# Three places in the instruction order of a gated-linear-attention and mixture-of-experts kernel: ScalarE's transposed input before the router's scale, its sixth chunk's heads before a scale, VectorE's keys before a normalised merge

## The reference

```
h  = layernorm(x)
q  = relu(h Wq)   16 heads of 64          k = relu(h Wk)   4 heads of 64      v = h Wv   4 heads of 64
g  = log_sigmoid(h Wg1 Wg2 + bg2) / 16    per key channel
S_t = exp(g_t) S_(t-1) + k_t v_t^T ;  o_t = (q_t / 8) S_t          (gated linear attention)
o  = g_norm_weight * o / rms(o) per head ;   x1 = x + layernorm(o Wo)
n  = layernorm(x1)
logits = n router_w^T + router_b ; the best 2 of 8 experts, gates = softmax of the two logits
y  = sum over the two experts e of gate_e * (silu(n gate_e^T) * (n up_e^T)) down_e^T
out = x1 + layernorm(y)
```

## Time and profile before

| | |
|---|---|
| time, median of 3 runs | 1233.63 us (1232.5 to 1234.02) |
| profiled execution, its time | 1234.89 us |
| its span, first to last instruction | 1233.1 us |
| mean granted TensorE clock | 0.983 |
| busy | PE 1159.7 us (94%), PEld 985.2 (80%), DVE 771.2 (63%), ACT 652.6 (53%), POOL 554.7 (45%) |
| first stage | to about 800 us, a turn every 48 us in the loop |

### The profile page before, as it was taken

The page is one execution under the profiler, slowest core; times in us unless marked ns, Lnnn a source line. Parts: engine busy times, 40 slices in busy tenths (PEclk is TensorE's granted clock), DMA queues, the critical chain, the costliest instruction groups (busy, mean ns, idle before and its releaser), DMA issues.

```text
span 1233.1 us, 29645 instructions
## 1 busy us (share of the span) xinstructions
PE 1159.7 (94%) x9166; PEld 985.2 (80%) x9166; DVE 771.2 (63%) x2380; ACT 652.6 (53%) x1653; POOL 554.7 (45%) x686
## 2 busy tenths in 40 slices
PE   8999999999999999999999999499999999999895
PEld 5878878878788788788788788379999999988762
DVE  5777777886887787777778868523333333333337
ACT  4755656557547557556565573334444444443336
POOL 2244464554654654644645544423333333333326
PEclk9999999999999999999999999689999999999998
DMA  7010110100101100101101001334111111111534
GB/s 280 10 28 14 30 43 9 34 28 24 34 17 30 38 17 26 43 13 30 43 9 34 28 15 43 135 106 116 49 46 51 49 45 51 47 48 43 175 118 189
DMA packets 59676, 67.50 MB, mean 55 GB/s; under 512 B 6896, under 2 KB 49664, under 8 KB 59264
## 3 DMA queue, kind: packets, MB, share of 16 engines
q1 hardware_dynamic: 48720, 41.10, 10.7%
q0 software_dynamic: 8448, 17.45, 4.3%
q10 hardware_dynamic: 2480, 8.61, 2.1%
HBM read 37.98 MB, written 29.15 MB: 54 GB/s over the span
## 4 chain that ended last, share of the span: by engine, by line
PE 65%; DVE 18%; issue 6%; ACT 6%; DMA 3%; DVEq 1%; POOL 0%; ACTq 0%; SPq 0%; POOLq 0%
PE pO L779 9%; PE pO L606 5%; PE pW L639 5%; PE pO L611 5%; PE pA L770 4%; PE pA L771 4%; PE pJ L770 4%; PE pJ L771 4%; PE pJ L561 3%; PE pA L590 3%; DVE qT L1133 3%; DVE ss L1181 3%; PE pJ L519 2%; PE pA L561 2%; PE pJ L639 2%
## 5 line engine op out<-in xcount | busy, mean ns | idle before, releaser
L1656 POOL DMA_INDIRECT expert_out<-y,tail x136 | 130.1, 957 | 263.3 <-ACT y L1038 239.8
L890 ACT ACTIVATE sq<-pO 128x512 f32<-128x512 f32 x128 | 75.8, 592 | 159.3 <-PE pO L606 109.0
L606 PEld LDWEIGHTS pO<-vJ,aT 128*128 128x128 f32 x1024 | 127.9, 192 | 27.0 <-issue 24.0
L606 PE MATMUL pO<-vJ,aT 128*128 128x128 f32 x1024 | 139.1, 279 | 5.5 <-DVE aT L1174 5.5
L1567 POOL DMA_INDIRECT expert_rows<-x1n,rowi x120 | 120.3, 1002 | 47.7 <-issue 29.5
L779 PE MATMUL pO<-wdown_sb,vJ 128*128 128x128 f32 x1088 | 134.1, 277 | 0.0
L1181 DVE TENSOR_REDUCE ss<-sq 128x8 f32<-128x512 f32 x128 | 86.4, 675 | 68.6 <-ACT sq L890 67.6
L779 PEld LDWEIGHTS pO<-wdown_sb,vJ 128*128 128x128 f32 x1088 | 128.4, 194 | 0.0
L1435 DVE TENSOR_TENSOR vJ<-pA,kJ 128x256 f32<-128x256 f32 x136 | 57.6, 425 | 108.3 <-ACT kJ L1027 108.3
L611 PE MATMUL pO<-S_mid,qT 128*128 128x128 f32 x896 | 118.3, 275 | 0.0
L611 PEld LDWEIGHTS pO<-S_mid,qT 128*128 128x128 f32 x896 | 109.1, 192 | 0.0
(11 more groups left out here) (234 smaller groups left out, 2422.5 us busy)
## 6 DMA issues: line engine op xcount, KB each, us to landing
xt<-expert_rows SPq DMA_DIRECT2D x69, 130.0 KB
xa<-x SPq DMA_DIRECT2D x16, 256.0 KB, 3.0
xr<-x SPq DMA_DIRECT2D x16, 256.0 KB, 2.9
after_attention<-x SPq DMA_DIRECT2D x16, 256.0 KB, 2.4
arena<-after_attention ACTq DMA_DIRECT2D x8, 512.0 KB
expert_rows<-zeros SPq DMA_DIRECT2D x8, 390.0 KB
expert_out<-y,tail POOLq DMA_INDIRECT x136
wgate_sb<-wgate SPq DMA_DIRECT2D x1, 2048.0 KB, 9.4
```

What stands on the lines that cost most here:

```text
L606: last = mm(o[:, g, h, :, :], aT[:, c % 2, h, g * P:(g + 1) * P], vJ[:, c, h, :], start=(h == 0 and g == 0), stop=(c == 0), skip_group_che ...
L1656: g.indirect_dma_start(out=ys_dram, in_=y[:, k, :], in_offset=None, out_offset=bass.IndirectOffsetOnAxis(ap=tail[:, k, 1:2].bitcast(U32), ...
```

## The change

Three edits, in the streams of ScalarE and VectorE. Nothing is added or taken away.

- In chunk 2, `norm_T(i + 1)` stands ahead of `router_rstd(i - 1)` instead of behind it.
- In chunk 6, `out_T(i, 5)` stands ahead of `head_scale(i, 6)` instead of behind it. This is in every sequence, the first and the last too.
- `keys(i + 1)` is called within chunk 7, behind `gate_steps(i + 1)` and ahead of the chunk's `merged_apply(i, 2)`, where it stood behind the whole of `chunks`.

```diff
@@ ScalarE: chunks
                         norm_rstd(i + 1)
+                    if more and c == 2:
+                        norm_T(i + 1)
                     if routed and c == (2 if more else 1):
                         router_rstd(i - 1, i - 1)
-                    if more and c == 2:
-                        norm_T(i + 1)
                     if c in (4, 6):
...
+                    if c == 6:
+                        out_T(i, c - 1)
                     head_scale(i, c)
-                    if c > 0:
+                    if c > 0 and c != 6:
                         out_T(i, c - 1)
@@ VectorE: chunks, and turn
                         gate_steps(i + 1)
+                        keys(i + 1)
                     if c in (4, 6, 7):
                         merged_apply(i, (4, 6, 7).index(c))
...
                 chunks(i, True, routed)
-                keys(i + 1)
                 key_rows(i + 1)
```

## The result

The changed kernel takes 1229.8 us (median of 7 runs, 1227.24 to 1230.56); the kernel before took 1234.02 (7 runs) beside it. The ratio is 0.9949, 95% interval 0.9935 to 0.9964: faster, but by 4 us, where 14.0 were forecast, and the time lies 2.3 us above the upper end of the range (1227.5). The profiled execution has a span of 1227.4 us (1233.1 before), with a mean granted clock of 0.984 (0.983).

The account below looks back on a forecast made before the run. TensorE's stream and its waits were taken to bound the kernel: 10.5 us (norm_T) plus 3.2 (keys less heads' copy) plus 0.45 less 0.2 made 14.0 us less, 1219.6 us from 1233.63; range 1212.5 to 1227.5.

Parts of the forecast that it names:

- Edit 1, 0.75 us a turn: Chunk 2: norm_T first removes TensorE's wait for xnT (0.65) and its restart (0.10), 0.75 us in each of 14 turns.
- Edit 2, 0.33: Chunk 6: the heads' copy put first delays ScalarE's scale and VectorE's run behind it, costing 0.33 us a turn.
- The forecast wait before L532: TensorE's 0.41 us wait before the merge in chunk 6 only moves to the keys' products, as a new short wait.
- 0.45 forecast: First sequence: no router competes for VectorE, so moving the heads' copy up gains 0.45 us.
- the 0.2 of the last sequence: Last sequence: moving the heads' copy costs between 0 and 0.33 us, taken as 0.2.
- Edit 3, 0.56: End of chunk 7: keys start 0.7 us sooner, of which TensorE's removed wait for them earns 0.56 us a turn.
- The cap that I named: End of the turn: ScalarE's values, ending at 402.4 just ahead of L573, let no more than 0.3 us net pass.
- Edits 2 and 3 cancel: Rival: the heads' copy and keys moves offset each other, leaving norm_T's 7.4 to 10.5 us: 1223 to 1226 us; 22%.
- slower: Rival: gains in chunk 2 and at L573 are eaten, leaving the heads' copy's cost: 1238 to 1240 us; 5%.
- Edit 2 was not free: Answers the rival that slack in chunks 6 and 7 hides the scale's delay: 18.3 us less, 1215 us; 10%.
- it bounds nothing: Answers the rival that another chain such as GpSimd's holds the turn at 47.97 us: 1233.6 us; 3%.
- the 1 to 2 us that the prediction set down for it: TensorE's clock drops and returns at another point in a shorter first stage: 1 to 2 us either way, in all cases.

Follow-up runs that it names:

- e8: The kernel before, none of the three edits, with one more 128x384 ScalarE copy ahead of the eight value copies: 1234.4 us in one run.
- e9: The changed kernel without the heads' copy moved in chunk 6, and with two of eight value copies done by VectorE: 1226.43 us, 0.9911 of before.
- e7: The changed kernel with 8 empty semaphore increments on TensorE right ahead of L573's wait: 1231.96 us in one run.

## Why the prediction was wrong

- **Edit 1, 0.75 us a turn: right.** L829 runs right behind the squares, L519 has no wait, L840 comes 3.06 us behind the squares instead of 3.70, 0.64 sooner (0.6 forecast). Alone it gave 0.80, and on top of edit 3 without the pauses also 0.80 (47.08 - 46.28, on two chips).
- **Edit 2, 0.33: right, a little high.** 0.27 alone, 0.26 on top of edits 1 and 3 (46.54 - 46.28, on two chips; 47.54 - 47.28). That is the price by spacing: L903 at 388.96, L895 at 389.53, 0.57 us for an instruction of 0.67. The Trainium skill (Perfetto Trace Analysis, Optimizing Scalar/DVE Operations) says that the write acknowledgement within a profiled duration overlaps with the next instruction; the 0.57 against 0.67 of this trace agree. The forecast wait before L532 is there, 0.62 us. The first sequence earned 0.46 by this edit alone (44.37 to 43.91 us from the first L573 to the second), 0.45 forecast; the 0.2 of the last sequence was not measured.
- **Edit 3, 0.56: this step failed.** TensorE's wait for the keys went as forecast (L539 to L546 0.52 sooner), but the step took it that a wait that is gone ahead of L546 is gone at the end of the turn. On the chips with pauses it is worth -0.12 instead of +0.56; where no pause is, 0.45 (first turn of the loop, 47.75 - 47.30) to 0.50 (47.58, worked out, - 47.08). The cap that I named, ScalarE's values at 402.4, was the wrong one: `e8` put them later at no cost and `e9` sooner with no gain.
- **Why the kernel before hid it.** From the first load of L622 in chunk 7 to the last of L573 it took 402.77 + 0.91 - 397.33 = 6.35 us before, 400.96 + 0.38 - 394.85 = 6.49 after, and 392.69 + 0.94 - 387.76 = 5.87 on the chip without the pause. In all nine profiled runs that have the pause, in every turn of the loop, the loads stop 5.5 to 5.65 us behind that load of L622 and go on at 5.95 to 6.1, whatever number of them had passed. In the kernel before, L573 started at 5.44, so that its 40th load came at about 5.44 + 0.91 x 39 / 56 = 6.07 (an estimate), no sooner than with the pause. So on the paused chips the last third of L573 doesn't come earlier, whether there is a wait for the keys (before: 0.36 us) or none. The wait lay beside the pause.
- **Sum.** 0.75 + 0.56 - 0.33 = 0.98 a turn was forecast. Without pauses it is 47.75 - 46.71 = 1.04 in the loop's first turn, and on the chip without them the time fell by 1229.9 - 1214.24 = 15.7 us (forecast 14.0). With them it is 0.44. That is 0.54 a turn too little, 7.6 us of the 9.8 that are missing; the rest is not followed further: the changed kernel started 1.2 us later, and the seven runs spread over 3.3 us.
- **The rivals.** "Edits 2 and 3 cancel" (1223 to 1226) comes nearest and was too kind: together they cost 0.36 (47.54 - 47.18) on the first chips. The mechanism I gave to "slower", a stop at L573 that eats edit 3's gain, was there, though not for the values. Edit 2 was not free. GpSimd had 1.45 us of idle time before S_mid, 2.13 before; it bounds nothing. The clock was 0.984 and 0.983, and no row or run gives the 1 to 2 us that the prediction set down for it.
- **What the profile of before could tell.** TensorE's stream had no pause marked at L573, and nothing in it told of one. But a stop behind the jump stood in it as VectorE's wait of 0.42 us for L590 in each turn, although L590 had ended 0.57 us before VectorE started. On the chips where that wait was gone the pause was gone too. I had not looked at it.

The version to keep depends on the chip: where the pauses are, edit 1 alone has the shortest turn (47.18 against 47.28 with edit 3 too), but the intervals of the two ratios overlap (0.9912 and 0.9938 in one job, 0.9903 and 0.9913 in another); where they are not, it is edits 1 and 3 (turn 46.28, 1210.21 us in one run with 8 idle increments). Edit 2 costs on both.

What stays open: what makes TensorE pause on some chips. Shown is that it is no semaphore of L573, that it takes the hardware loop as well as the chip or its job (L573 outside the loop has no pause in any run), that 8 instructions right ahead of it move it by three loads (one run) and 8 in chunk 3 don't, and that the pause in L573 and VectorE's wait behind the jump went together, on both chips that lacked them. Both fit a stream whose next instructions come late in a loop, but nothing here measured that.

## What to carry to other kernels

A wait that is removed is worth what the next limit leaves of it, and that limit can be a pause for which the profile names no cause, and which no row shows while the wait covers it; here it took all of the gain of a wait ahead of 56 short matmuls. Look for a wait behind a matmul that had long ended, and compare the loop with the part of it that is written out: here L573 had no pause there, and the stretch from it into the loop's first turn gave the edits' worth without the pause, on the same chip. And a gain of half a per cent that one chip shows or denies should be tried on another: here the same three edits gave 0.9949 on one and 0.9868 on another.

## What was not expected of the hardware

- Chips of the same kind differ: the kernel before took 1234.0 to 1236.7 us in five jobs and 1228.4 (one run) and 1229.9 in two, 0.3 to 0.7% less, at the same mean clock. In the kernel before, 14 waits of 0.4 us behind the loop's jump would account for 5.6 us of it.
- The pause in L573 stands behind the 36th to 40th of 56 loads (behind the 34th to 36th in `e7`), is 0.3 to 0.5 us long, and is over 5.95 to 6.1 us behind the first load of L622 in chunk 7, in every version that has it. It is in all 14 L573 of the hardware loop and in neither of the two outside it.
- 8 empty increments on TensorE cost nothing in chunk 3 (47.96 against 47.98) or ahead of L573; 24 of them made the turn 1.8 us longer (48.09 against 46.28, one run each).
